# One decoder layer on one core: the PSUM ring numbered through all batches, and the second head's scores issued one product behind the first's

## The reference, cut to what matters

```python
q = (x @ Wq + bq).reshape(b, lq, H, D)          # 256 rows, 16 heads of 64
k = (embeds @ Wk + bk).reshape(b, lk, H, D)     # 1601 keys
v = (embeds @ Wv + bv).reshape(b, lk, H, D)
scores = jnp.einsum('bqhd,bkhd->bhqk', q, k) * SCALE
attn = jax.nn.softmax(scores, axis=-1)
ctx = jnp.einsum('bhqk,bkhd->bqhd', attn, v).reshape(b, lq, AD)
return ctx @ Wo + bo
```

## Time and profile before

| | us |
|---|---|
| median of 3 runs | 3011.64 (3011.18 to 3011.82) |
| the profiled execution | 3014.56 |
| its span in the trace | 3012.8 |
| PE busy | 2792.6 (93%) |
| PE weight loads busy | 2313.8 (77%) |
| DVE, ACT, POOL busy | 2213.8, 1689.9, 2125.0 |

### The profile page before, as it was taken

The page is one execution under the profiler, slowest core; times in us unless marked ns, Lnnn a source line. Parts: engine busy times, 40 slices in busy tenths (PEclk is TensorE's granted clock), DMA queues, the critical chain, the costliest instruction groups (busy, mean ns, idle before and its releaser), DMA issues.

```text
span 3012.8 us, 71520 instructions
## 1 busy us (share of the span) xinstructions
PE 2792.6 (93%) x28504; PEld 2313.8 (77%) x28504; DVE 2213.8 (73%) x4113; ACT 1689.9 (56%) x3422; POOL 2125.0 (71%) x1708
## 2 busy tenths in 40 slices
PE   5799999999999999999999999999999999997371
PEld 3588888888888888888888888888888888886250
DVE  6778787878778788778788777878787777874104
ACT  2466665656656666656566666656566666663020
POOL 2377777777777777777777777777777777786305
PEclk8799999999999999999999999999999999998586
DMA  3100000000000000000000000000000000000022
GB/s 95 44 2 12 2 13 2 13 2 12 2 2 12 2 13 2 13 2 13 2 13 2 2 13 2 13 2 13 2 13 2 27 2 2 2 2 1 23 92 63
DMA packets 65328, 40.71 MB, mean 14 GB/s; under 512 B 6615, under 2 KB 62636, under 8 KB 65011
## 3 DMA queue, kind: packets, MB, share of 16 engines
q1 hardware_dynamic: 62962, 32.35, 3.7%
q0 software_dynamic: 2048, 3.91, 0.5%
HBM read 28.15 MB, written 8.39 MB: 12 GB/s over the span
## 4 chain that ended last, share of the span: by engine, by line
PE 89%; issue 5%; POOL 3%; DVE 1%; ACT 1%; DMA 0%; POOLq 0%; DVEq 0%; ACTq 0%
PE ps L1330 28%; PE ps L1342 24%; PE ps L1304 7%; PE ps L1293 4%; PE ps L1295 3%; PE ps L1294 3%; PE ps L1279 3%; PE ps L1277 3%; PE ps L1278 3%; PE ps L1351 2%; PE ps L1360 2%; PE ps L1284 2%; PE ps L1450 1%; PE ps L1457 1%; PE ps L1312 1%
## 5 line engine op out<-in xcount | busy, mean ns | idle before, releaser
L600 POOL TENSOR_TENSOR key_sums<-key_sums,prob_T 128x512 f32<-128x512 f32 (+1 forms) x1408 | 1811.0, 1286 | 162.4 <-POOL key_sums L600 1.8
L991 DVE TENSOR_REDUCE mx<-ps 128x1 f32<-128x400 f32 (+1 forms) x2048 | 1069.9, 570 | 454.5 <-PE ps L1304 416.0
L763 ACT ACTIVATE prob_T<-ps 128x512 f32<-128x512 f32 x1536 | 833.6, 596 | 212.9 <-PE ps L1330 192.4
L1342 PE MATMUL ps<-prob_T,v_sb 128*64 128x256 f32 (+1 forms) x6656 | 742.4, 380 | 1.1 <-ACT prob_T L766 1.1
L1342 PEld LDWEIGHTS ps<-prob_T,v_sb 128*64 128x64 f32 (+1 forms) x6656 | 478.4, 137 | 243.7 <-issue 2.1
L1330 PE MATMUL ps<-shift,shift_w 64*128 64x256 f32 (+1 forms) x3328 | 504.8, 299 | 1.6 <-ACT prob_T L763 1.2
L596 POOL TENSOR_TENSOR key_sums<-prob_T 128x512 f32<-128x512 f32 x128 | 165.8, 1295 | 476.8 <-ACT prob_T L763 476.8
L1330 PE MATMUL ps<-q_hi,k_hi 64*128 64x256 f32 (+1 forms) x3328 | 470.4, 278 | 0.0
L1330 PE MATMUL ps<-q_lo,k_hi 64*128 64x256 f32 (+1 forms) x3328 | 468.4, 277 | 0.0
L1330 PE MATMUL ps<-q_hi,k_lo 64*128 64x256 f32 (+1 forms) x3328 | 467.7, 277 | 0.0
L752 ACT COPY heads_raw<-ps 128x256 f32<-128x256 f32 x128 | 47.8, 373 | 672.8 <-PE ps L1342 672.8
(11 more groups left out here) (173 smaller groups left out, 3632.2 us busy)
## 6 DMA issues: line engine op xcount, KB each, us to landing
ctx_raw<-in_ctx_dram SPq DMA_DIRECT2D x16, 768.0 KB
tables<-in_L_ffn_W_dram SPq DMA_DIRECT2D x16, 256.0 KB, 3.8
slots_in<-zeros SPq DMA_DIRECT2D x32, 64.0 KB
xs<-in_x_dram SPq DMA_DIRECT2D x8, 256.0 KB, 3.2
xres<-in_x_dram SPq DMA_DIRECT2D x8, 256.0 KB, 3.0
v_sb<-slots_in SPq DMA_DIRECT2D x8, 256.0 KB, 2.8
slots_out<-v_sb SPq DMA_DIRECT2D x8, 256.0 KB, 4.0
out_dram<-x1s SPq DMA_DIRECT2D x8, 256.0 KB
```

The lines of the kernel that those rows point to most:

```text
L600: op = nc.gpsimd.tensor_tensor(acc[0:rows, :, :], acc[0:rows, :, :], prob_T[0:rows, :, k, :], ALU.add)
L763: nc.scalar.activation(prob_T[:, h, 2 * i:2 * i + 2, :].rearrange("p k t -> p (k t)"), ps[:, bank, :], ACT.Exp).then_inc(ring_act, 1)
L991: v.tensor_reduce(mx[:, qt, h, c:c + 1], ps[:, at.bank("mx", r, c, qt, h), 0:WID[c]], AX.X, ALU.max).then_inc(ring_dve, 1)
L1342: last = mm(ps[h * DH:h * DH + DH, bank, 0:T], v_sb[0:rows, r % NJ // 2 % 2, k, v0 + h * DH:v0 + h * DH + DH], prob_T[0:rows, h, k, :], st ...
```

## The change

It does two things. The banks are numbered by the count of all fills since the start of the program, so a fill always takes the bank of the eighth fill before it, at the borders of batches too. And the order in a unit is new. With a0 to a7 for head 0's eight score products, b0 to b7 for head 1's, and m0, m1 for the two maxima, before it was

    m0 m1 | a0 b0 a1 b1 a2 b2 a3 b3 a4 b4 a5 b5 a6 b6 a7 b7

and it becomes

    a0 m1 a1 b0 a2 b1 a3 b2 a4 b3 a5 b4 a6 b5 a7 b6 m0 b7

Each of the four banks is now asked for on its own, just ahead of a0, m1, b0 and m0; `maximum` takes one head, with its two waits for keys and queries each time. The ring's order becomes: scores of head 0, maxima of head 1, scores of head 1, maxima of head 0. The products, their shapes, and what ACT, DVE and POOL compute are the same; DVE reduces head 1 ahead of head 0.

```diff
     for s in range(SLOTS_A_BATCH):
         following, after = s < 7 or more, s < 6 or more
         for i, unit in enumerate(MAX_UNITS):
+            if i < UNITS:
+                put("act", "s", s, i, 0)
             if following:
-                maximum(s + 1, unit)
+                maximum(s + 1, unit, 1)
             if i < UNITS:
-                for h in range(2):
-                    put("act", "s", s, i, h)
+                put("act", "s", s, i, 1)
+            if following:
+                maximum(s + 1, unit, 0)
...
     def bank(self, *key):
-        return bank_at(self.kind, PLACE[self.kind][key])
...
+        return RING[(self._count("all fills", *self.find(*key)) - 1) % len(RING)]
 
     def held_by(self, *key):
 
-        place = PLACE[self.kind][key]
-        if place >= len(RING):
-            return True, place - len(RING)
-        kind = BEFORE[self.kind]
-        bank = bank_at(self.kind, place)
-        return False, max(i for i in range(len(FILLS[kind])) if bank_at(kind, i) == bank)
+        place = PLACE[self.kind][key] - len(RING)
+        return (True, place) if place >= 0 else (False, place + len(FILLS[self.before]))
...
             def maxima(at, r, units):
                 for c, qt in units:
-                    for h in range(2):
+                    for h in (1, 0):
...
-            def maximum(at, r, c, qt):
+            def maximum(at, r, c, qt, h):
                 pe.wait_ge(kh_ok, at.n(4, r, c + 1))
                 pe.wait_ge(qh_ok, at.n(1, r, 1))
-                banks = banks_of(at, *[("mx", r, c, qt, h) for h in range(2)])
-                for h in range(2):
-                    lanes = slice(h * DH, h * DH + DH)
-                    mm(ps[:, banks[h], 0:WID[c]], q_hi[r % 2][lanes, qt * P:qt * P + P],
-                       k_hi[r % 2][lanes, KEY0[c]:KEY0[c] + WID[c]], start=True, stop=True).then_inc(rows_full[h], 1)
+                bank, lanes = bank_of(at, "mx", r, c, qt, h), slice(h * DH, h * DH + DH)
+                mm(ps[:, bank, 0:WID[c]], q_hi[r % 2][lanes, qt * P:qt * P + P],
+                   k_hi[r % 2][lanes, KEY0[c]:KEY0[c] + WID[c]], start=True, stop=True).then_inc(rows_full[h], 1)
...
+            def score_unit(at, s, i, unit):
+
                 tiles = [k for k in (2 * i, 2 * i + 1) if k < KT]
-                rows = P if i < UNITS - 1 else KREM
-                for n, k in enumerate(tiles):
...
+                steps = [(n, k, step) for n, k in enumerate(tiles) for step in range(4)]
+
+                first, = banks_of(at, ("s", s, i, 0), also=[("k", s, 3), ("q", s), ("sh", s)] if i == 0 else [])
+                for at_step, part in enumerate(steps):
+                    ahead = score_step(s, 0, first, *part)
+                    if at_step == 0:
+                        if unit:
+                            maximum(at, s + 1, *unit, 1)
+                        second = bank_of(at, "s", s, i, 1)
+                    else:
+                        score_step(s, 1, second, *steps[at_step - 1])
+                ahead.then_inc(rows_full[0], 1)
+                if unit:
+                    maximum(at, s + 1, *unit, 0)
+                score_step(s, 1, second, *steps[-1]).then_inc(rows_full[1], 1)
```

More of the change, by code:

```diff
@@ L72, in batch_fills, with maximum @@
     put = lambda owner, *key: fills.append((key, owner))
-    def maximum(r, unit):
-        for h in range(2):
-            put("dve", "mx", r, *unit, h)
+    def maximum(r, unit, h):
+        put("dve", "mx", r, *unit, h)
     if kind == "start":
@@ L86, in batch_fills @@
         for unit in MAX_UNITS:
-            maximum(0, unit)
+            maximum(0, unit, 1)
+            maximum(0, unit, 0)
         for c in range(4):
@@ L126 @@
 FILLS = {kind: batch_fills(kind) for kind in ("start", "first", "mid", "last", "end")}
-BEFORE = {"first": "start", "mid": "mid", "last": "mid", "end": "last"}
 PLACE = {kind: {key: i for i, (key, _) in enumerate(f)} for kind, f in FILLS.items()}
@@ L133, in owned @@
     owners, makers = [o for _, o in fills], [maker(key) for key, _ in fills]
-    return {"act": owners.count("act"), "dve": owners.count("dve"), **{m: makers.count(m) for m in MAKERS}}
-def bank_at(kind, place):
-    return RING[(place - len(FILLS[kind])) % len(RING)]
+    return {"all fills": len(fills), "act": owners.count("act"), "dve": owners.count("dve"),
+            **{m: makers.count(m) for m in MAKERS}}
 class Batch:
@@ L146, in __init__ @@
         self.kind, self.b = kind, b
[L147 to L157, removed]
+        phases = {"start": [], "first": ["start"], "mid": ["start", "first"] + ["mid"] * (b - 1),
+                  "last": ["start", "first"] + ["mid"] * (batches - 2)}
+        phases["end"] = phases["last"] + ["last"]
+        before = phases[kind]
+        self.before = before[-1] if before else None
+        self.start = {of: sum(owned(k)[of] for k in before) for of in owned("start")}
     def n(self, a_pair, s, c):
@@ L166, in find @@
             return True, PLACE[self.kind][key]
-        kind = BEFORE[self.kind]
-        if kind != "start":
+        if self.before != "start":
             key = (key[0], key[1] + (4 if key[0] == "v" else SLOTS_A_BATCH), *key[2:])
-        return False, PLACE[kind][key]
+        return False, PLACE[self.before][key]
     def _kind(self, own):
-        return self.kind if own else BEFORE[self.kind]
+        return self.kind if own else self.before
     def _count(self, of, own, place):
         here = owned(self._kind(own), place + 1)[of]
-        return self.start[of] + (here if own else here - owned(self._kind(own))[of])
+        return self.start[of] + (here if own else here - owned(self.before)[of])
     def full(self, *key):
@@ L751, in heads_out @@
                 act.wait_ge(ring_full, at.full("pv", r))
-                copy(heads_raw[:, :], ps[:, at.place_of("pv", r), 0:T]).then_inc(ring_act, 1)
+                copy(heads_raw[:, :], ps[:, at.bank("pv", r), 0:T]).then_inc(ring_act, 1)
             def exps(at, s, i):
@@ L994, in row_shift @@
             def row_shift(at, r, qt):
-                _, count = at.freed("mx", r, 3, qt, 1)
+                _, count = at.freed("mx", r, 3, qt, 0)
                 dve.wait_ge(ring_dve, count)
@@ L1313, in row_shift @@
                 last.then_inc(ring_full, 1)
-            def score_unit(at, s, i):
-                banks = banks_of(at, *[("s", s, i, h) for h in range(2)],
-                                 also=[("k", s, 3), ("q", s), ("sh", s)] if i == 0 else [])
-                tiles = [k for k in (2 * i, 2 * i + 1) if k < KT]
-                rows = P if i < UNITS - 1 else KREM
-                for n, k in enumerate(tiles):
[L1323 to L1333, removed]
@@ new lines, in score_step @@
+            def score_step(s, h, bank, n, k, step):
+                rows = P if k < KT - 1 else KREM
+                lanes, cols = slice(h * DH, h * DH + DH), slice(k * P, k * P + rows)
+                keys_part = (shift_w[lanes, 0:rows], k_hi[s % 2][lanes, cols], k_hi[s % 2][lanes, cols],
+                             k_lo[s % 2][lanes, cols])[step]
+                query_part = (shift, q_hi[s % 2], q_lo[s % 2], q_hi[s % 2])[step]
+                return mm(ps[0:rows, bank, n * T:n * T + T], keys_part, query_part[lanes, :],
+                          start=(step == 0), stop=(step == 3))
@@ L1368, in batch @@
                     for i, unit in enumerate(MAX_UNITS):
-                        if following:
-                            maximum(at, s + 1, *unit)
                         if i < UNITS:
-                            score_unit(at, s, i)
+                            score_unit(at, s, i, unit if following else None)
+                        elif following:
+                            maximum(at, s + 1, *unit, 1)
+                            maximum(at, s + 1, *unit, 0)
                     if s == 6 and more:
@@ L1403, in _ @@
             for unit in MAX_UNITS:
-                maximum(at, 0, *unit)
+                maximum(at, 0, *unit, 1)
+                maximum(at, 0, *unit, 0)
             for c in range(4):
```

5 lines of the change are left out of this document (removed).

## The result

| us | before | changed |
|---|---|---|
| median, 7 runs each | 3011.82 (3009.32 to 3012.31) | 3001.03 (2999.21 to 3001.95) |
| span in the trace | 3012.8 | 2998.2 |
| PE busy, PE loads busy | 2792.6, 2313.8 | 2794.4, 2339.5 |

What follows compares the result with a forecast made beforehand. PE was taken to bound the kernel, through its stalls. 127 slots x 0.18 = 22.9 us, plus 11.3 at borders, made 34.2: 3011.64 to 2977.5 us, with an 8-in-10 range of 2958 to 3021.

Steps and rivals of the forecast that it cites:

- The bound, and the loop through two banks: Attention units: PE sets the time; asking for both banks makes two units take 2.42 us, where PE alone needs 2.24.
- Numbering the banks: Batch borders: counting all fills through removes the first products' wait for the copy of the heads, -11.3 us.
- PE's pace in the new order: Attention units: the array's halves run on their own, 1.12 us a unit, bounded by 1.12 and 1.42.
- In step: Rival, attention units: unequal pairs wait for the longer partner, 1.19 us a unit, 3019 us in all; chance 0.20.
- no sharing: Rival, attention units: unequal products don't share the array, 1.42 us a unit, 3195 us in all; chance 0.12.
- The new order in the ring: Attention units: long stalls go, head 1's bank is 0.05 us late, holding b0 alone; 0.18 a slot, 22.9 us won.
- the wait moves: Rival, units 2 to 5: b0's wait holds everything behind it, four times 0.05 us; 3000 us in all; chance 0.11.
- The extra wait for keys and queries: Between a0 and m1 of each unit: one more wait instruction, 0 to 0.11 us at a slot's start, taken as 0.03.
- The tail: Slot's last units: unit 5's exponentials hold unit 7's m1 and the values' load, 8.14 us against 8.32; 0.18 of 0.6 won.
- The values' wait is a switch of the array, not ACT: First values product: its load waits because the tiling mode goes from 64 to 128 rows; the sum is unchanged otherwise.
- own range: Whole kernel: 2960 us if a slot gains 0.30 us, to 2996 if it gains 0.03.

Runs made afterwards that it cites:

- e3: The changed kernel with the wait for head 1's score bank moved behind a1, just ahead of b0; 2977.09 us, ratio 0.9875 to the kernel before.
- e6: The kernel before's product order, banks numbered by all fills, head 1's score bank asked for separately between a0 and b0; 2967.47 us, ratio 0.9855.
- e1: The kernel before with only the changed bank numbering, products in the old order; 3001.41 us, ratio 0.9956.
- e4: As e3, with the unit of maxima that has no scores beside it moved from a slot's end to its head; 2936.30 us, ratio 0.9738.
- e5: As e1, with the unit of maxima that has no scores beside it at the head of a slot; 2996.05 us, ratio 0.9951.
- e9: As e6, with the unit of maxima that has no scores beside it at the head of a slot; 2979.14 us, ratio 0.9898.
- e7: As e4, but with the wait for head 1's score bank ahead of a1, as in the changed kernel; 2952.75 us, ratio 0.9804.

## Why the prediction was right or wrong

*The bound, and the loop through two banks.* Right. e3 and e6 win by loosening just that.

*Numbering the banks, -11.3.* Right: 0.9956 for the numbering alone, which is 13 us (9 to 17), and -10.8 us for the whole change.

*PE's pace in the new order, 1.12 a unit.* Right: 1.12 to 1.13 for an undisturbed unit in the changed kernel and in e3 (medians). "In step" and "no sharing" are out.

*The new order in the ring, -22.9.* **Wrong, and this is the step that failed.** "b0 alone is held by it, while a0 and a1 run": the release time was right (I had 2.35 us after the earlier unit's a0; unit 0 gives 2.36, from 1183.04, its a0 with the 0.11 of the open load, to 1185.40), but the point where it was due was read from the ring's order instead of from the place of the wait in the program. It is due at a1's load, 0.06 us earlier, and whatever is late there holds both halves. Two stalls of 0.08 a slot, at units 2 and 4, ate the gain: 0.17 of the 0.18. Moving the wait behind a1 brings it back: load at 8.17, about 24 us under e1 (e3). The rival "the wait moves" had the time, 3000, and half the mechanism: it held everything behind the wait, but put the wait at b0 and shared the loss out over four units at 0.05, where it is two at 0.08. It had a chance of 0.11.

*The extra wait for keys and queries.* Nothing to be seen of it: e3's load is at 8.17 with everything counted, against 8.14, and the first a0 and m1 of a slot begin together (both at 1182.93 in the changed kernel).

*The tail.* Right in its place and its cause: m1 of unit 7 is held by unit 5's exponential (load 0.11 after its end in every slot; e3 against e4, 41 us), and the values' load by the next one. That one was put at 8.02 and ends at 8.04 in e3; the load follows 0.13 later, where the sum had 0.04. I gave it as a cost of the change, and did not see that moving one unit of maxima takes it away.

*The values' wait is a switch of the array, not ACT.* Right for the kernel before; e5 and e9 show it, where the values' bank isn't ACT's at all. In the changed kernel ACT holds the load a further 0.08, as the sum's timing by ACT's end allowed.

*Two small slips.* The six reductions of the earlier trace rows give 0.55 us a piece, waits included, not 0.49; back to back DVE does take 0.48 (e9). That DVE costs nothing holds for the changed kernel, and not for e9. And a slot gain of 0.30 gives 2962, not 2960.

The range of 2958 to 3021 held the result; the narrower "own range" of 2960 to 2996 did not. The best kernel of the study is e4: 2.6% under the kernel before, 2.3% under the changed one.

## What to carry to other kernels

Where an in-order engine has other work to issue, a wait belongs straight ahead of the first instruction that needs it: here each product of distance cost 0.16 us a slot, 0.7 to 0.9% of the kernel. After a change that splits a resource in halves, the idle column no longer tells a stall: measure from start to start. And a new order of issue in a ring also changes which engine holds which bank. That brought the changed kernel its wait in the tail, and e9 its wait for DVE; list, for each fill, the eighth fill before it, before costing an order. The two fixes, of the wait's place and of the tail, each paid with or without the other (0.9 and 0.7% for the wait, 1.6 and 1.4% for the tail, in the table at e7).

## What the runs showed of the hardware

The halves of the array run at their own pace, as long as no wait in PE's instruction stream holds them both. Products of 400 and 256 columns run beside each other with no loss (1.13 us a unit, as with equal pairs), and a half that has been held stays behind: 0.11 to 0.13 us through units 2 to 6 in e6. More than that: at 1186.45 the changed kernel's m1 of unit 3 starts 0.07 ahead of that unit's a0 at 1186.52, though a0 is the earlier instruction. Head 0's half still had the 400 columns of m0 then; here a product started ahead of an earlier one that waited for the other half. The Trainium skill, TensorE: Matmul & The Clock Gate, "The mechanism", has matmuls strictly in program order at their start; in this trace, where two row tiles are out of step, the recorded starts are not.
